# Grouped cross attention in two passes of eight heads, with split float32r products and normalised probabilities

## The reference

```python
q = rms_norm((x @ Wq).reshape(B, 256, 16, 128), q_norm_w)   # 16 heads
k = rms_norm((ctx @ Wk).reshape(B, 256, 4, 128), k_norm_w)  # 4 groups of 4 heads
v = (ctx @ Wv).reshape(B, 256, 4, 128)
probs = softmax(q @ k.T / sqrt(128))                        # per head, k and v repeated
x = layernorm(x + (probs @ v).reshape(B, 256, 2048) @ Wo)
```

## Time and profile before

| | |
|---|---|
| runs, median (lowest to highest) | 3919.83 us (3917.16 to 3927.21) |
| the profiled execution, span | 3915.1 us (the profile gives no time beyond its span) |
| PE, PEld, DVE, ACT, POOL busy | 84%, 49%, 43%, 30%, 6% |
| mean granted TensorE clock | 0.943 |
| grouped cross attention, first DMA to last store | 2341.70 to 3316.95 us |

### The profile page before, as it was taken

How to read it: one execution, slowest core, us unless ns; L and a number is a source line. 1 busy time by engine, 2 the same in 40 slices (tenths; PEclk the granted TensorE clock), 3 DMA queues, 4 the chain that set the end, 5 groups by cost and what they waited for, 6 DMA issues and landing times. The chain is left out here.

```text
span 3915.1 us, 45980 instructions
## 1 busy us (share of the span) xinstructions
PE 3308.1 (84%) x15122; PEld 1924.5 (49%) x15123; DVE 1672.6 (43%) x3287; ACT 1159.5 (30%) x3024; POOL 238.9 (6%) x205
## 2 busy tenths in 40 slices
PE   6999667788876699999788878999999998799894
PEld 5666412222221567777555545555665555444441
DVE  5666646666665212112166653333443333211113
ACT  2333224445444111111044433323343332211110
POOL 1000100000000200000100000000000001300002
PEclk9999879989898799999899999999999999999997
DMA  1000264444440300000100003000000000700323
GB/s 65 22 16 17 58 89 76 71 70 70 70 70 27 104 17 17 12 11 17 41 14 28 23 31 115 17 17 11 7 17 17 12 6 26 271 17 32 118 78 113
DMA packets 113094, 186.93 MB, mean 48 GB/s; under 512 B 8840, under 2 KB 53352, under 8 KB 112912
## 3 DMA queue, kind: packets, MB, share of 16 engines
q1 hardware_dynamic: 92032, 135.40, 14.3%
q0 software_dynamic: 7664, 27.40, 2.0%
q10 hardware_dynamic: 13216, 21.82, 1.6%
HBM read 130.10 MB, written 54.10 MB: 47 GB/s over the span
## 5 line engine op out<-in xcount | busy, mean ns | idle before, releaser
L1143 DVE TENSOR_REDUCE x_minus_max<-banks 128x2 f32<-128x1024 f32 x256 | 308.6, 1221 | 176.4 <-PE banks L1251 173.3
L1088 ACT ACTIVATE x_probs<-banks 128x512 f32<-128x512 f32 x512 | 290.9, 596 | 278.8 <-PE banks L1269 206.1
L1269 PE MATMUL banks<-x_stacked_q,x_stacked_k 105*128 105x512 bf16 x512 | 207.9, 416 | 83.0 <-ACT x_probs L1088 59.8
L476 ACT ACTIVATE a_probs<-banks,a_minus_max 128x128 f32<-128x128 f32 (+1 forms) x512 | 209.0, 426 | 145.0 <-DVE a_minus_max L559 143.3
L1984 PE MATMUL banks<-x_w_q,x_xT 128*128 128x512 f32 x512 | 232.6, 600 | 17.3 <-ACT x_xT L1856 17.3
L1251 PE MATMUL banks<-x_stacked_k,x_stacked_q 102*128 102x512 bf16 x512 | 171.5, 420 | 85.3 <-DMA x_stacked_k<-x_mask_parts_dram 60.5
L2090 PE MATMUL banks<-x_w_o,x_ctxT 128*128 128x512 f32 x512 | 221.0, 592 | 0.0
L1880 ACT ACTIVATE x_probs<-banks,x_minus_max,x_rroot 128x256 f32<-128x256 f32 x256 | 142.3, 560 | 204.1 <-DVE x_minus_max L1941 204.1
L1269 PEld LDWEIGHTS banks<-x_stacked_q,x_stacked_k 105*128 105x128 bf16 x512 | 50.4, 100 | 302.4 <-ACT x_probs L1088 194.0
L559 DVE TENSOR_REDUCE a_minus_max<-banks 128x2 f32<-128x512 f32 (+1 forms) x192 | 131.7, 686 | 82.3 <-PE banks L709 62.2
L2421 DVE TENSOR_TENSOR m_h<-banks,m_silu 128x512 f32<-128x512 f32 x39 | 27.0, 692 | 318.7 <-PE banks L2537 166.6
(11 more groups left out here) (347 smaller groups left out, 6431.9 us busy)
## 6 DMA issues: line engine op xcount, KB each, us to landing
x_parts_dram<-x_parts SPq DMA_DIRECT2D x16, 768.0 KB, 9.2
x_stacked_q<-x_parts_dram SPq DMA_DIRECT2D x48, 256.0 KB
x_stacked_k<-x_parts_dram SPq DMA_DIRECT2D x48, 256.0 KB
x_after<-a_z SPq DMA_DIRECT2D x16, 512.0 KB, 2.8
x_x<-x_after SPq DMA_DIRECT2D x16, 512.0 KB, 5.4
x_after<-x_z SPq DMA_DIRECT2D x16, 512.0 KB, 2.9
m_w<-in_m_g SPq DMA_DIRECT2D x8, 1024.0 KB, 5.7
m_w<-in_m_u SPq DMA_DIRECT2D x8, 1024.0 KB, 9.0
```

What stands on the lines that cost most here:

```text
L476: ins = act.activation(probs[:, n % 3, i * width:(i + 1) * width], psum[uses.bank(use)][:, i * width:(i + 1) * width], ACT.Exp, bias=minus ...
L1088: act.activation(probs[:, n % 8, :], psum[at.bank(f"exp{n}")], ACT.Exp, scale=SCALE)\
L1143: dve.tensor_reduce(minus_max[:, c % 2, h % 4, 2 * (n % 2):2 * (n % 2) + 2], at.pair(use), AX.X, ALU.max, negate=True)\
L1269: ins = pe.matmul(psum[at.bank(use)], stacked[1][u][:, h, s * P:(s + 1) * P], stacked[0][u][:, h, :], start=True, stop=True)
```

## The change

The stage walks through all batches twice. Pass 0 does heads 0 to 7 (two groups) and adds its half of the output product to x, which goes to a DRAM tensor `half_way`; pass 1 does heads 8 to 15, loads `half_way`, adds, and does the norm. One batch in one pass is a unit; there are 16. `every_unit` walks them as: front of unit 0, then for each pass one opening pair, a loop over two pairs, and a closing pair. The front of the following unit (transposes of x, products k and v) is done inside a unit, behind its last scores.

Every product goes through `split_matmul`, so each operand exists as high part and rest. Weights arrive in ten chunks of 128x2048 over two raw buffers; ACT rounds a chunk and DVE subtracts (`round_chunk`, `rest_of_chunk`). Chunks 0 and 1 are split in the front, the others after fixed steps of units 0, 7 and 8 (`chunk_at`). PSUM results that are operands later (xT, v, kT, qT, transposed probabilities, contexts) are rounded out of PSUM by ACT and subtracted out of PSUM by DVE, which frees the bank. POOL splits the context and multiplies the probabilities by the reciprocals in SBUF, before they are transposed; the spread reciprocals, their transposes and copies are gone. Transposes stand 3 steps behind the scores and contexts 4 (`T_LAG`, `O_LAG`), where it was 1 and 2.

```diff
+HALVES = 2; GH = G // HALVES; HH = H // HALVES      # 2 groups, 8 heads
+T_LAG = 3
+O_LAG = 4
...
 PE
+                for n in range(HH + O_LAG):
+                    if n < HH:                       # scores n, 2 x split_matmul
...
+                    if n < 2:
+                        q_group(own, 1, n)
+                    elif n < 4:
+                        transpose_q(own, 1, n - 2)
+                    if T_LAG <= n < HH + T_LAG:
+                        h, use = n - T_LAG, f"T{n - T_LAG}"
+                        wait_bank(pe, own, use)
+                        pe.wait_ge(normalised, own.w * HH + (h + 1))
...
+                    if n == HH and following:
+                        transpose_x(following)
+                    if HH < n < HH + 3 and following:
+                        context_product(following, n - HH - 1)
+                    if n >= O_LAG:
+                        h, use = n - O_LAG, f"O{n - O_LAG}"
+                        wait_bank(pe, own, use)
+                        wait_free(pe, own, f"T{h}")
...
 ACT
+                for n in range(HH + O_LAG):
+                    if n < HH:
+                        exps(own, n)
+                    if n < 2:
+                        q_out(own, 1, n)
+                    elif n < 4:
+                        qT_out(own, 1, n - 2)
+                    if T_LAG <= n < HH + T_LAG:
+                        use = f"T{n - T_LAG}"
+                        wait_full(act, own, use)
+                        high_part_act(act, probsT[0][...], psum[...]).then_inc(probs_rounded, 1)
...
+                    if n >= O_LAG:
+                        wait_full(act, own, f"O{n - O_LAG}")
+                        high_part_act(act, ctxT[0][...], psum[...]).then_inc(ctx_rounded, 1)
+                    if (k := chunk_at(own, n)) is not None:
+                        round_chunk(k)
...
 DVE
+                for n in range(HH + O_LAG):
+                    if n < HH:
+                        row_maxima(own, n)           # reduce, then minus_max
+                    if n < 2:
+                        q_sums(own, 1, n)
...
+                    elif n < 4:
+                        rest_of_qT(own, 1, n - 2)
+                    if 1 <= n <= HH:
+                        dve.reciprocal(inverse[:, n - 1, :], sums[:, n - 1, :]).then_inc(inverse_ready, 1)
+                    if T_LAG <= n < HH + T_LAG:
+                        dve.wait_ge(probs_rounded, own.w * HH + (h + 1))
+                        subtract(dve, probsT[1][...], psum[...], probsT[0][...]).then_inc(free[...], 1)
+                    if n == HH and following:
+                        rest_of_xT(following)
+                    if n == HH + 1 and following:
+                        k_sums(following)
+                    if n == HH + 2 and following:
+                        rest_of_v(following)
+                    if n >= O_LAG:
+                        dve.wait_ge(ctx_rounded, own.w * HH + (h + 1))
+                        subtract(dve, ctxT[1][...], psum[...], ctxT[0][...]).then_inc(free[...], 1)
+                    if (k := chunk_at(own, n)) is not None:
+                        rest_of_chunk(k)
...
 POOL
+                root(own, 1, 2)
+                root(own, 2, 3)
+                for s in range(HH):
+                    normalise(own, s)                # tensor_tensor and tensor_scalar, 128x256
+                    if following and s < KC:
+                        split_context(following, s)  # copy and subtract, 128x256
...
+        core.release_semaphores()
+        cross_attention_grouped(core, "x1", between[3], a["ctxT"], between[4], half_way, ...)
```

More of the change, by code:

```diff
@@ L88, in high_part, with high_part_act @@
     return engine.tensor_copy(out.bitcast(F32R), x)
+def high_part_act(act, out, x):
+    return act.copy(out.bitcast(F32R), x)
 def subtract(engine, out, x, part):
@@ L1742, in sem @@
             return core.semaphore(f"{name}_{tag}")
[L1744 to L1748, removed]
+        raw = sb("raw", [P, 2, CHUNK])
+        w_kv = [sb(f"w_kv_{part}", [P, 2, KC, GH * HD]) for part in ("high", "rest")]
+        w_q = [sb(f"w_q_{part}", [P, GH, KC, HG * HD]) for part in ("high", "rest")]
+        w_o = [sb(f"w_o_{part}", [P, HH, D]) for part in ("high", "rest")]
@@ L1760, in cross_attention_grouped @@
[L1760 to L1771, removed]
@@ L1772, in cross_attention_grouped @@
-        kv_weights = sem("kv_weights")
-        o_weights = sem("o_weights")
-        gain_ready = sem("gain_ready")
-        context_loaded = [sem(f"context_loaded{u}") for u in range(2)]
+        x = sb("x", [P, 2, TT, D])
+        context = sb("context", [P, KC, S1])
+        ctx_parts = [sb(f"context_{part}", [P, KC, S1]) for part in ("high", "rest")]
+        xT = [sb(f"xT_{part}", [P, KC, T]) for part in ("high", "rest")]
+        squares = sb("squares", [P, 3, 512])
+        square_sums = sb("square_sums", [P, 1 + GH, 8])
@@ new lines, in cross_attention_grouped @@
+        probs = sb("probs", [P, 4, TT, S1])
+        probsT = [sb(f"probsT_{part}", [P, 2, TT, T]) for part in ("high", "rest")]
+        sums = sb("sums", [P, HH, TT])
+        inverse = sb("inverse", [P, HH, TT])
+        ctxT = [sb(f"ctxT_{part}", [P, HH, T]) for part in ("high", "rest")]
+        stats = sb("stats", [P, TT, 6])
+        moments = sb("moments", [P, TT, 2])
+        vareps = sb("vareps", [P, TT])
+        rstd = sb("rstd", [P, TT])
+        x_loaded = [sem(f"x_loaded{u}") for u in range(2)]
@@ L1807, in _, with root @@
+            every_unit(sp, front, sequence)
         @block.gpsimd
         def _(pool):
[L1809 to L1816, removed]
+            def root(own, part, n):
+                pool.wait_ge(mean_ready, own.w * 3 + n)
+                cols = slice(0, 4 if part == 0 else 8)
+                pool.tensor_tensor(rroot[:, part, cols], mean_squares[:, part, cols], core.minus_half[:, cols], ALU.pow).then_inc(rroot_ready, 1)
@@ new lines, in _, with round_chunk, square @@
+            act.dma_start(gains[:, 0:1], weights["qn"].rearrange("(p a) -> p a", a=1)).then_inc(gains_loaded, 16)
+            act.dma_start(gains[:, 1:2], weights["kn"].rearrange("(p a) -> p a", a=1)).then_inc(gains_loaded, 16)
+            def round_chunk(k):
+                act.wait_ge(raw_loaded[k % 2], sum(32 if i % CHUNKS == 0 else 16 for i in range(k % 2, k + 1, 2)))
+                high_part_act(act, chunk_of(split_weights, k, 0), raw[:, k % 2, :]).then_inc(w_rounded, 1)
+            def square(own, use, n):
+                wait_full(act, own, use)
+                if not (n == 0 and isinstance(own.w, int) and own.w == 0):
+                    act.wait_ge(summed, own.w * 5 + (0, 1, 1, 2, 3)[n])
+                return act.activation(squares[:, n % 3, :], psum[own.bank(use)][:, :], ACT.Square).then_inc(squared, 1)
@@ new lines, in exps @@
+            def exps(own, s):
+                bank = psum[own.bank(f"S{s}")]
+                act.wait_ge(max_ready, own.w * HH + (s + 1))
+                for t in range(TT):
+                    at = (s % HG) * TT + t
+                    ins = act.activation(probs[:, s % 4, t, :], bank[:, t * S1:(t + 1) * S1], ACT.Exp,
+                                         bias=minus_max[:, s, t:t + 1], scale=rroot[:, 1 + s // HG, at:at + 1],
+                                         accum_out=sums[:, s, t:t + 1])
+                ins.then_inc(free[own.bank(f"S{s}")], 1)
@@ new lines, in front, with q_group @@
+            def front(own):
+                transpose_x(own)
+                context_product(own, 0)
+                context_product(own, 1)
+            def q_group(own, g, t):
+                use = f"q{g}_{t}"
+                wait_bank(pe, own, use)
+                pe.wait_ge(x_split, own.w + 1)
+                wait_chunk(own, 2 + g)
+                for c in range(KC):
+                    ins = split_matmul(pe, psum[own.bank(use)][:, :], [part[:, c, t * P:(t + 1) * P] for part in xT],
+                                       [part[:, g, c, :] for part in w_q], start=c == 0, stop=c == KC - 1)
+                done(ins, own, use)
```

736 lines of the change are left out of this document (447 added, 289 removed).

## The result

| | median (lowest to highest), us | runs | ratio to before, 95% interval |
|---|---|---|---|
| before | 3923.52 (3917.16 to 3927.45) | 4 | |
| after | 3988.98 (3986.24 to 3994.18) | 4 | 1.0171 (1.0156 to 1.0186) |

The change makes the kernel 65 us slower; forecast were 88 us (4008 us, range 3938 to 4075). The profiled execution of after has a span of 3992.3 us, 77.2 more than before. Of that, 13.1 lie ahead of the changed stage: the last store before it is issued at 2351.61 instead of 2338.50, in stages that the change doesn't touch. Such stretches move from one execution to the next, so stages are compared from store to store: 978.45 us before, 1044.14 after, 65.7 us more, as the runs say.

What follows compares the result with a forecast made beforehand. A ring of DVE and ACT waiting for each other was taken to set the pace, with PE waiting. The stage summed 6 + 23 + 982 + 22 + 6 + 27 - 6 + 4 = 1064 against 975.3 us: 4008 us, range 3938 to 4075.

Steps and rivals of the forecast that it cites:

- The step: One head in units' steps 4 to 7: DVE and ACT wait for each other in a ring, 3.66 us against 2.82 before.
- The plain unit: One batch in one pass, from its first q instruction to the output product's end: 61.4 us, sixteen times 982 us.
- (a): POOL's work in mid-unit delays DVE's minus_max, which has two SBUF inputs: 1.4 us a unit, 22 in all.
- (b): PE's granted clock falls in the steps, which lose nothing; the k product behind may double: 0.4 us a unit, 6 in all.
- (c): Eight weight chunks rounded on ACT and subtracted on DVE inside the ring: 3.4 us each, 27 in all.
- (d): Release of some 65 semaphores between the previous stage's last store and this stage: 6 us, bounds 2 and 8.
- (e): Stage start to first q product: two chunks land in 10 us, then roundings and k and v products; 23 us.
- (f): The last unit has no following unit whose front it must do: -6 us.
- Tail: Stage end, from the last product to the store: stays 4 us.
- Rival 1: PE stays the bound because the queues run ahead further: units of 50 us, 3826 us; chance 0.11, with otherwise faster cases.
- Rival 3: Ring right but links shorter, no collisions, chunks half hidden: 60 us a unit, 3939 us; chance 0.09.
- Rival 4: Split products do not run at 0.118 and 0.233 us in this stage; chance almost nothing.

Runs made afterwards that it cites:

- e1: Changed kernel, with ACT taking the high parts of transposed probabilities and contexts ahead of the exponentials from step 2 on: 3901.82 us, ratio 0.9955 to before.
- e2: Changed kernel with ACT's high parts ahead of the exponentials from step 2 and POOL's context splits moved between its two roots: 3859.68 us, ratio 0.9839 to before.
- e4: Changed kernel with one of three split products left out in scores and contexts, 512 instructions fewer: 3983.40 us, ratio 1.0161 to before.
- e9: Changed kernel with POOL's context splits moved and only the transposed probabilities' high part ahead of the exponentials, the contexts' behind: 3889.15 us, ratio 0.9921 to before.
- e3: Changed kernel with only POOL's context splits moved out of the first heads, ACT's order kept: 3983.56 us, ratio 1.0151 to before.
- e11: Changed kernel with DVE subtracting the x transposes ahead of the second weight chunk at the front: first q product at 22.7 instead of 25.6 us; one run, 3971.8 us.

## Why the prediction was right, and which terms were mis-sized

The sign and the mechanism were right, shown by e1, e2, e4 and e9 together with the links of the step: a ring of the DVE and ACT queues, in which TensorE waits. Term by term, forecast and then measured:

- The step: 3.66 us; 3.55 where nothing collides. The sum was 0.1 too high, mostly since the exponentials start 0.20 us after minus_max, not 0.28.
- The plain unit: 61.4 us; 60.7 in e3, where no context part lengthens a step, in the half of its plain units in which the clock costs nothing. Sixteen units give 11 us less than forecast.
- (a) Contention: 22 us; about 9, 0.55 a unit (61.3 against e3's 60.7). This is the largest error. Minus_max lasts 0.23 us on average against 0.16: 0.07 x 8 = 0.56 a unit, the same number. The forecast's 0.9 us for the power never came; minus_max 2 ran inside it at its usual length, in 15 of the 16 units. Of the 128 minus_max, 27 began while GpSimd subtracted a context part, and they took 0.37 to 0.66 us. In the timeline of after:

```profile
3105.63 1.64 POOL L1976 TENSOR_TENSOR x_rroot<-x_mean_squares,minus_half 128x8 f32<-128x8 f32 x1 [8.94 <-DVE x_mean_squares L2128]
3106.26 0.16 DVE L2184 SCALAR_TENSOR_TENSOR x_minus_max<-x_row_max,x_rroot 128x2 f32<-128x2 f32 x1
...
3109.18 0.73 POOL L98 TENSOR_TENSOR x_context_rest<-x_context,x_context_high 128x256 fp32r<-128x256 f32 x1
3109.55 0.38 DVE L2184 SCALAR_TENSOR_TENSOR x_minus_max<-x_row_max,x_rroot 128x2 f32<-128x2 f32 x1
```

  Beside a context part it did wait, until that one's end, 0.2 us.
- (b) Clock: 6 us; about 2, one unit of 63.0. It does fall in the ring, to 0.50, and costs nothing there, as forecast.
- (c) Chunks: 27 us; 13.4 in unit 0, 7.2 and 6.8 in units 7 and 8, 27.4. That the total fits is partly luck. Six chunks inside the ring lengthen their steps by 3.0 to 3.7 us, as priced. Chunk 2, ahead of unit 0's first step, costs some 5.3 (row maximum 0 comes 2.7 us later than in other units, row maximum 1 another 2.6), and chunk 7, behind the last scores, under 1.
- (d) Release: 6 us; 5.2. (e) Front: 23 us; 25.6, of which 2.9 are the contention of e11. The 10 us for the landing of two chunks had no row; the second chunk's rounding started 11.8 us after the first DMA. I had looked for that lock only in the loop, not where large subtractions meet GpSimd.
- (f) Last unit: -6; -3.8 (57.5 us). Tail 4; 4.0.

From the first q product to the last product's end that is 1006 us against 1031, the whole stage 1041 against 1064. Step, contention and clock were together 28 us too high, front and last unit 5 too low, so the total is nearer than its terms. The forecast median was 19 us too high: these 23, less the 4 by which the median of before is higher in the new runs (3923.5, not 3919.8). Two of the signs that were named didn't come. PE was busy for 83% of a plain unit and idle for 10 us, not 75% and 15: its own work is 47.8 us at full clock (e2) instead of 46, and the lower clock stretches it to 51. And the plain units took 61.3 us, not 62 to 64.

Rival 1 (TensorE the bound) failed for the changed order. Its point of decision was set too low: 55.8 us was worked out as level, but e1, with units of 56.0, is 18 us faster than before. The 55.8 counts the 28 us of (a) and (b) beside the units, while a measured unit contains them; without them level is (975.3 - 54) / 16 = 57.6. Its 50 us a unit is nearly what e2 reaches (52.6). Rival 3 (60 a unit, 3939) named the right direction of the error, with links shorter and collisions rarer, but too far. Rival 4 is out: the split products start 0.233 and 0.118 us apart.

## What to carry to other kernels

When two in-order queues hand work to each other in both directions within one step, add up the chain once around; if it exceeds each engine's own work, it is the pace, whatever the busiest engine saves. Putting the instruction whose input was oldest first in one queue was worth 85 us here, and 130 with the third queue cleared, against 65 lost by the change. Inside this ring the waiting engine's lower clock cost nothing, and work saved on it gained nothing.

## What the runs showed of the hardware

- The granted clock fell to 0.50 where PE waited much (3.7 us steps) and stayed at 1.00 in most units when these waits were gone (e2). With fewer products for the same waits (e4) four plain units instead of one were longer for a low clock, by 1.5 to 2.1 us. That took back 7 of the 10 us that leaving the products out had saved in the twelve plain units.
- A scalar-times-row instruction on GpSimd, 128x256, took 0.94 us, the tensor-by-tensor form of the same shape 0.63 (L1994 and L1993 of after, 128 each).
- Clearing some 65 semaphores costs 5.2 us between two stages, 0.08 us each.
